# Early expert tiles spread over the stream's closing events, and the first late rows sent ahead of the last early stores

## The reference, cut to what matters

```python
for w, g, b, s in zip(conv_ws, ln_gs, ln_bs, strides):      # 7 convolutions, each with layer norm and gelu
    h = gelu(layernorm(conv1d(h, w, s)))
h = layernorm(h) @ proj_w + proj_b                          # 8 x 374 tokens of 192
h = h + ssm(layernorm(h))                                   # a state space layer, a scan over the tokens
v = layernorm(h)
expert = argmax(softmax(v @ gate_w + gate_b - center))      # one of 4 experts for each token
h = h + (gelu(v @ w1[expert] + b1[expert]) @ w2[expert] + b2[expert])
```

## Time and profile before

| | |
|---|---|
| median of 3 runs | 2250.69 us (2245.63 to 2251.97) |
| the profiled execution, its own time | 2253.02 us |
| its span | 2251.2 us |
| PE busy | 2112.5 us, 94% of the span |
| DVE, ACT, POOL busy | 59%, 49%, 38% |
| mean granted clock of PE | 0.973 of full speed |

### The profile page before, as it was taken

One profiled execution on the slowest core, in us unless ns is written; L12 is line 12 of the kernel. 1 busy time (PEld: TensorE's weight loads), 2 busy tenths in 40 slices (PEclk: granted clock), 3 DMA queues, 4 the chain that ended last, 5 costly groups with the idle time before them and its releaser, 6 DMA issues. The chain is left out here.

```text
span 2251.2 us, 40813 instructions
## 1 busy us (share of the span) xinstructions
PE 2112.5 (94%) x14347; PEld 1897.5 (84%) x14347; DVE 1329.3 (59%) x3454; ACT 1112.1 (49%) x2104; POOL 857.5 (38%) x767
## 2 busy tenths in 40 slices
PE   6999999999999999999999999597979889979998
PEld 5889999999999999999999988487956567769998
DVE  5776667667667667667666765333358567652223
ACT  4556655555555555555565554132335366653320
POOL 4445555555565565455455553110143000100100
PEclk9999999999999999999999999699989899989999
DMA  9400000000000000000000020133510011129966
GB/s 270 154 4 4 5 4 4 5 9 4 5 9 4 3 9 4 4 9 4 4 9 4 1 60 10 60 91 107 147 25 21 21 42 56 69 81 320 333 212 246
DMA packets 97333, 137.15 MB, mean 61 GB/s; under 512 B 14036, under 2 KB 77694, under 8 KB 96507
## 3 DMA queue, kind: packets, MB, share of 16 engines
q1 hardware_dynamic: 75146, 105.18, 14.9%
q10 hardware_dynamic: 15664, 18.69, 2.4%
q0 software_dynamic: 6336, 10.85, 1.7%
HBM read 89.14 MB, written 45.50 MB: 60 GB/s over the span
## 5 line engine op out<-in xcount | busy, mean ns | idle before, releaser
L506 POOL TENSOR_TENSOR t_rstd<-t_var,t_minus_half 128x4 f32<-128x4 f32 (+1 forms) x379 | 367.0, 968 | 632.6 <-DVE t_var L426 631.1
L317 PE MATMUL banks<-t_wt,t_l 128*128 128x256 f32 (+1 forms) x2836 | 598.9, 350 | 0.0
L317 PEld LDWEIGHTS banks<-t_wt,t_l 128*128 128x128 f32 x2836 | 510.8, 192 | 52.7
L380 ACT ACTIVATE t_sq<-banks 128x512 f32<-128x512 f32 (+1 forms) x379 | 215.9, 570 | 569.4 <-PE banks L317 567.9
L434 DVE TENSOR_TENSOR t_yn<-banks,t_rstd 128x512 f32<-128x512 f32 (+1 forms) x379 | 249.0, 657 | 368.1 <-POOL t_rstd L506 366.9
L308 PE MATMUL banks<-t_wt,t_l 128*128 128x128 f32 x2836 | 385.5, 278 | 4.3 <-ACT t_l L398 2.9
L308 PEld LDWEIGHTS banks<-t_wt,t_l 128*128 128x128 f32 x2836 | 354.9, 193 | 14.6 <-ACT t_l L398 4.1
L512 POOL TENSOR_TENSOR t_zrstd<-t_zvar,t_minus_half 128x8 f32<-128x8 f32 x188 | 307.6, 1637 | 12.2 <-DVE t_zvar L470 12.2
L414 ACT ACTIVATE t_l<-banks,t_cols 128x512 f32<-128x512 f32 x376 | 286.3, 777 | 27.9 <-PE banks L370 24.4
L398 ACT ACTIVATE t_l<-banks,t_cols 128x512 f32<-128x512 f32 (+1 forms) x381 | 284.8, 747 | 12.7 <-PE banks L330 7.3
L423 DVE TENSOR_REDUCE t_ss<-t_sq 128x4 f32<-128x512 f32 (+1 forms) x379 | 244.7, 646 | 77.6 <-ACT t_sq L380 70.2
(11 more groups left out here) (382 smaller groups left out, 3340.8 us busy)
## 6 DMA issues: line engine op xcount, KB each, us to landing
t_w_rest<-in_w SPq DMA_DIRECT2D x48, 480.0 KB
ect<-t_ECT SPq DMA_DIRECT2D x16, 750.0 KB, 3.2
t_l<-in_w1a SPq DMA_DIRECT2D x27, 384.0 KB, 3.8
sorted_by_expert<-t_h SPq DMA_DIRECT2D x4, 2400.0 KB
routed_by_expert<-t_h SPq DMA_DIRECT2D x4, 2400.0 KB
t_w_first<-in_w SPq DMA_DIRECT2D x16, 480.0 KB
t_ectb<-ect ACTq DMA_DIRECT2D x5, 1500.0 KB, 7.9
ys<-t_ye ACTq DMA_DIRECT2D x64, 96.0 KB
```

The lines of the kernel that those rows point to most:

```text
L317: mm = pe.matmul(psY[bank][:, t * C:end * C], src[:, at:at + P], weights[:, C:(1 + end - t) * C], start=False, stop=(t + 1 == n))
L380: act.activation(T["sq"][:, par, 0:n], psY[bank][:, 0:n], ACT.Square).then_inc(S["squared"], 1)
L506: pool.tensor_tensor(T["rstd"][:, par, 0:n], T["var"][:, par, 0:n], T["minus_half"][:, 0:n], ALU.pow)\
```

## The change

1. `piece_at` reads a table. Pieces 0 to 10 go to places 1 to 11: after the second and third closing event and after steps 27 to 35 of batch 6. The next 21 pieces (11 to 31) are spread over the 36 steps of batch 7, at steps 0, 1, 3, 5, 6, 8, 10, 12, 13, 15, 17, 18, 20, 22, 24, 25, 27, 29, 30, 32 and 34. The last ten (32 to 41) follow.
2. `pool_loop_over` moves ahead, into the last chunk behind the root of its event 4, and waits for the layer-1 products of that chunk alone.
3. SP sends the rows of tiles 0 to 5 and `w2` at once after `loop_over`, and `b2` only after the last event of the loop.
4. SP's loop over the tiles runs on without a break: for tiles 14 to 19 too the order is weights, rows, and the store of the tile six before. The six stores of tiles 8 to 13, which were all ahead of tile 14's weights, are now behind the rows of tiles 14 to 19, one each.

```diff
@@ -1070,10 +1070,18 @@
     HALF_H = HID // 2
     PIECES, PHI_SUMS, PHI_SCALE = 3, 7, 10
     PLACES = len(TAIL) + CHAIN - (LEFT + len(TAIL)) + CHAIN
-    FIRST_PLACE = 12
+
+
+
+    FIRST_PLACE, LAST_CHAIN, BEHIND = 1, PLACES - CHAIN, 10
+    FILL = LAST_CHAIN - FIRST_PLACE
+    AMID = PIECES * EARLY - BEHIND - FILL
+    PIECE_PLACES = [FIRST_PLACE + k for k in range(FILL)] + [LAST_CHAIN + n * CHAIN // AMID for n in range(AMID)] \
+        + [PLACES + n for n in range(BEHIND)]
+    piece_of = {place: k for k, place in enumerate(PIECE_PLACES)}
 
     def piece_at(place):
-        return place - FIRST_PLACE
+        return piece_of.get(place, -1)
 
     def pe_rows(pe, i):
         pe.wait_ge(S[f"rows_loaded{i % FFN_RING}"], 16 * (i // FFN_RING + 1))
@@ -1229,31 +1237,25 @@
         for i in range(FFN_RING):
             sp_weights(sp, i)
         sp.wait_ge(S["loop_over"], 1)
-        sp.dma_start(b2[:, :], bass.AP(io["b2"].tensor, 0, [[0, P], [1, N_EXPERT * D]])).then_inc(S["b2_loaded"], 16)
         sp.wait_ge(S["scattered"], 16 * TPB * EARLY_BATCHES)
         for i in range(FFN_RING):
             sp_rows(sp, i)
             if i < N_EXPERT:
                 w = slice(i * HC * D, (i + 1) * HC * D)
                 sp.dma_start(w2[:, w], io["w2"][:, w]).then_inc(S["w2_loaded"], 16)
-        for i in range(FFN_RING, EARLY):
+        sp.wait_ge(S["conv_done"], END)
+        sp.dma_start(b2[:, :], bass.AP(io["b2"].tensor, 0, [[0, P], [1, N_EXPERT * D]])).then_inc(S["b2_loaded"], 16)
+
+        for i in range(FFN_RING, ROUTED):
+            if i == EARLY:
+                sp.wait_ge(S["list_ready"], 2)
             sp_weights(sp, i)
+            if i == EARLY:
+                sp.wait_ge(S["scattered_late"], 16 * TPB * (B - EARLY_BATCHES))
             sp_rows(sp, i)
             sp_store(sp, i - FFN_RING)
-        for i in range(EARLY - FFN_RING, EARLY):
-            sp_store(sp, i)
-        sp.wait_ge(S["list_ready"], 2)
-        sp_weights(sp, EARLY)
-        sp.wait_ge(S["scattered_late"], 16 * TPB * (B - EARLY_BATCHES))
-        for i in range(EARLY, EARLY + FFN_RING):
-            if i > EARLY:
-                sp_weights(sp, i)
-            sp_rows(sp, i)
-        sp_soft(sp)
-        for i in range(EARLY + FFN_RING, ROUTED):
-            sp_weights(sp, i)
-            sp_rows(sp, i)
-            sp_store(sp, i - FFN_RING)
+            if i == EARLY + FFN_RING - 1:
+                sp_soft(sp)
         for i in range(ROUTED - FFN_RING, ROUTED):
             sp_store(sp, i)
         for r in range(OUT_RING):
@@ -1290,9 +1292,8 @@
 
     def pool_loop_over(pool):
 
-        pool.wait_ge(S["conv_done"], END)
-        pool.wait_ge(S["normed"], END)
-        pool.wait_ge(S["h_ready"], END - LAG)
+
+        pool.wait_ge(S["conv_done"], count(CHUNKS - 1, 3))
         pool.wait_ge(S["l0_ready"], 8 * CHUNKS)
         pool.wait_ge(S["l0_done"], 8 * CHUNKS)
         pool.wait_ge(S["patch_turned"], 2 * CHUNKS)
@@ -1379,7 +1380,7 @@
             for step in range(CHAIN):
                 pe_chain(pe, B - 1, step)
                 pe_piece(pe, piece_at(CHAIN - LEFT + step), 0, EARLY)
-            for place in range(PLACES, FIRST_PLACE + PIECES * EARLY):
+            for place in range(PLACES, PLACES + BEHIND):
                 pe_piece(pe, piece_at(place), 0, EARLY)
             for k in range(PIECES * (ROUTED - EARLY)):
                 pe_piece(pe, k, EARLY, ROUTED)
...
@@ -1496,11 +1497,11 @@
                     root(pool, event(j, g))
                     if 2 <= g <= 5 and j + 2 < CHUNKS:
                         patch_root(pool, j + 2, g - 2)
+                    if j == CHUNKS - 1 and g == 4:
+                        pool_loop_over(pool)
                     pool_chain(pool, *chain_at(j, g))
             for n, e in enumerate(TAIL):
                 root(pool, e)
-                if n == 0:
-                    pool_loop_over(pool)
                 pool_chain(pool, B - 2, LEFT + n)
             for step in range(LEFT + len(TAIL), CHAIN):
                 pool_chain(pool, B - 2, step)
```

## The result

| | before | after |
|---|---|---|
| median | 2250.29 us (6 runs) | 2234.90 us (6 runs, 2234.03 to 2240.0) |
| span of the profiled execution | 2251.2 us | 2232.8 us |
| mean granted clock of PE | 0.973 | 0.981 |
| ratio, after to before | | 0.9937 [0.9927, 0.9947] |

A forecast was written before the change was run, and what follows sets the result against it. Short waiting steps bound the closing stretch, TensorE's work batch 7, then a hole precedes tile 14. Terms 7.5 - 17.4 - 2.5 - 2.2 = -14.6 us from the 2250.7 median gave 2236 us, range 2229 to 2246.

The forecast's parts named there:

- closing stretch: 1435 to 1461 us, end of batch 6's chain: eleven pieces go in, 26.0 us becomes 33.5, +7.5.
- batch 7 to the ranks: 1461.0 to 1540.4 us: fewer pieces but more uncovered waits, 79.4 us becomes 62.0, -17.4.
- ranks to tile 14's rows: 1540.4 to 1565.13 us: ten pieces and no 7.19 us hole, 24.7 us becomes 22.2, -2.5.
- first late tiles: From tile 14's rows to the first late down: at full clock 9.7 us becomes 7.5, -2.2.
- What bounds the kernel: Closing stretch bound by short steps waiting for one another; batch 7 by TensorE's work, busy 73.7 of 79.4 us.
- the stretch might stay at half clock: Rival for the closing stretch: half clock to its end, +21 in place of +7.5, 2250 us; chance 0.10.
- the wait of 2.25: Behind the ranks, TensorE waits for DVE's copy queued behind the late-tile list: 2.5 us predicted, 2.25 before.
- 2 us to spare: Behind the ranks: tile 8's store leaves at about 11.5 us, lands about 2 later; tile 11's sum due at 15.7.
- The terms costed at nothing: POOL's clears and `loop_over` ahead, early `w2` and row loads, later `b2`: no cost.
- The clock lost in batch 7: Rival: batch 7's waits drop TensorE to half clock for the whole stretch, 2275 us; chance 0.04.
- the clock that goes up and down: Rival in batch 7: about a third of the work at half clock gives back 13 us, 2249 us; chance 0.07.
- Late rows: Rival at tile 14: rows arrive some 4 us after need, about +6, 2242 us; chance 0.08.

The follow-up runs named there:

- e2: Kernel before with only SP's new order (tile 14's weights and rows ahead of the stores of tiles 8 to 13); ratio to before 0.9988.
- e4: Changed kernel with six pieces behind the steps in place of ten, 25 over batch 7; ratio to the kernel before 0.9972.
- e6: e4 with the stores of tiles 8 and 9 sent between tile 14's weights and the wait for the scatter; ratio to the kernel before 0.9978.
- e3: Kernel before with `loop_over`, the row loads and `w2` early, and `b2` later; ratio to the kernel before 1.0001.
- e10: Changed kernel with only `sp_soft`'s loads moved ahead of SP's wait for the list of late tiles; ratio to the kernel before 0.994.
- e12: Changed kernel with 16 pieces behind the steps in place of ten, 15 left over batch 7; ratio to the kernel before 0.9995.
- e8: Changed kernel with 22 pieces behind the steps in place of ten, 9 left over batch 7; ratio to the kernel before 1.0074.
- e7: Changed kernel with added, unused identity transposes in TensorE's waits of the last two loop events and the closing events; ratio to the kernel before 0.9916.
- e5: e2 with the stores of tiles 8 and 9 sent between tile 14's weights and the wait for the scatter; ratio to the kernel before 0.9973.

## Why the prediction was right, step by step

| term | predicted | measured, profiled executions |
|---|---|---|
| closing stretch | 33.5 us, +7.5 | 30.7, +4.6 |
| batch 7 to the ranks | 62.0, -17.4 | 62.1, -17.3 |
| ranks to tile 14's rows | 22.2, -2.5 | 22.2, -2.5 |
| first late tiles | 7.5, -2.2 | 8.1, -1.6 |
| sum | -14.6 | -16.8 |

The spans differ by 18.4: 0.95 lies ahead of the first row (1434.07 against 1435.02), 0.7 behind the last. The time was forecast as 2236 and is 2234.9. That it came so near is in part luck: between the two profiled executions, of which the sum was made, the gain was 3.8 us more than forecast, and the profiled execution of the kernel before took 2.7 us more than the median of all.

**What bounds the kernel** held: what each stretch takes is TensorE's work plus the waits that no piece covers. For batch 7, 49.7 us of work and 12.3 of waits were predicted, 50.6 and 11.5 measured.

**The closing stretch** was sized 2.8 us too high, by two items. The first is the clock. "I take the clock to be back after piece 1": it was back already from about 1438 us, in the third event's own matmuls, fell in the wait of 2.37, and was back for good within piece 1 at 1445.22. TensorE's work took 25.9 us, not 28.1. The second is the waits, which were 4.8 us, not 5.4: 0.42 for v where 1.1 stood. That the stretch might stay at half clock had 0.10 and did not come about: 0.99 from 1445.22 on.

**Ranks to tile 14's rows** held as predicted: DVE's work on the list, the wait of 2.25 (2.5 predicted), ten pieces. The rows left 10.3 us after the ranks, so SP's part was early by the 9 us of the text. But "by it DVE's sum of tile 11", with "2 us to spare", names one of three. The sum of tile 11 ran at 1542.77, as soon as its product was there; e2 and e4 show that the stores of tiles 8, 9 and 10 are one queue, 4 us apart, with the sums of 11, 12, 13 and the copy of tile 14 behind them. The number was right, since ten pieces cover the queue, and the reason was too short. SP in the changed kernel, the store of tile 10, and DVE, the sum of tile 13:

```profile
1546.59 0.36 SPq L1220 DMA_DIRECT2D routed_by_expert<-t_rout  x1
```
```profile
1549.35 0.36 DVE L1181 TENSOR_TENSOR t_rout<-banks,t_wt 128x192 f32<-128x192 f32 x1 [1.59 <-PE banks L1124]
```

The sum starts 2.8 us after the store was sent. In e2 a sum started 1.9 to 2.7 us after the sending of the store that it waited for, so here less than 1 us was to spare, and not 2. That the whole queue just fitted was not worked out. With the short reason I mispriced e4, and for e6 I overlooked SP's sends a second time, at tile 20.

**First late tiles**: waits of 0.89 and 0.74 us, where 0.74 stood twice; four ups and three pairs of transposes take the other 6.5, where 0.66 + 5.36 = 6.0 stood. A pair of transposes with nothing right behind it takes 0.38 to its end (1549.04 to the start of the wait of 0.89), not 0.22.

**The terms costed at nothing**, the clears and `loop_over` ahead, the early loads and the later `b2`: e3 shows them to be worth nothing in the kernel before. That the place of `sp_soft` costs nothing in the changed kernel, e10 shows.

**The rivals.** The clock lost in batch 7 is a real mechanism, and the place where it starts lies closer than a chance of 0.04 for the full loss suggests: with 20 pieces up to the ranks the clock stayed up (1.00), with 15 the whole gain was gone (0.92, ratio 0.9995), with 9 the kernel was slower than before (0.73, ratio 1.0074, 14.3 us of half clock). For the clock that goes up and down, the Trainium skill's section "A second HAM failure mode: psum-queue depth-cycling" in "TensorE: Matmul & The Clock Gate" has frequent short idle times make it do so. The trace of the changed kernel does not show it (1.00 with waits of up to 1.6 us), e12 and e8 do (0.92 and 0.73, with waits of up to 2.8 and 4.2 us), and e7 has one such fall with the changed kernel's own waits (0.97, 1.8 us). So the wait of 2.25 us that left the clock up, which the prediction held against that rival, did not rule it out; that the changed kernel kept 1.00 throughout is in part luck. Late rows: the scatter's semaphore let SP go by 1537.14, so that rival fell.

## What to carry over

When filler work is moved from a stretch where it is the bound into one where the engine waits, price both sides as work plus uncovered waits, and stop where the uncovered waits grow faster per piece, or where the clock falls in the trace. Here 14 pieces could leave batch 7, 19 took the gain away and 25 made the kernel slower. When a queue's sends are reordered, list every send that now stands behind the moved one, with its consumer and how much TensorE work lies ahead of that consumer: the slack found at the first need (2 us) said nothing of the third store or of the seventh late tile. And the two halves of a change, timed alone, may not add up to it.

## What the runs showed of the hardware

When the clock comes back is not a matter of the kernel's instructions alone. e2 and e5 send the same to TensorE up to batch 7, yet the granted clock from 1435 to 1461 us was 0.50 in e2's profiled execution and 0.63 in e5's, and batch 7 began 4.3 us earlier there (1456.36 against 1460.65). They ran on different chips; what decides it was not found. Batch 7 has the same instructions in e7 and in the changed kernel, and a clock of 0.97 and 1.00 there.

The executions of one kernel differ in it too. e12 went from 2242.4 us at a mean clock of 0.979 to 2254.9 at 0.975 over eleven runs, e5 from 2235.9 at 0.978 to 2247.1 at 0.973 over ten; e10, at 0.980 to 0.982, only from 2235.4 to 2236.0 over five.

Transposes of the identity, whose results nothing reads, keep the clock up: with them it read 1.00 from 1410 to 1457.7 us, against 0.81 without.
